# A post-norm decoder layer on one core: heads rotated and mixed in pairs, the rotated sum and its low part moved to GpSimd

## What is computed

```
x = layernorm(x + attention(x))      # 16 query heads, 4 key/value heads of 128, rotary q and k,
                                     # causal softmax, output projection Wo
x = layernorm(x + wkv(x, ctx))       # a scan along the 256 rows: running max, two decayed sums
x = layernorm(x + ffn(x))            # dense 512x512 plus top-2 of 16 rank-16 experts
```

## Time and profile before

| | |
|---|---|
| time, median of 3 runs | 1857.01 us (1853.22 to 1861.23) |
| the profiled execution's own time | 1865.38 us |
| its span, first to last instruction | 1863.6 us |
| mean granted TensorE clock | 0.962 |
| matmuls in the span | 11648 |

### The profile page before, as it was taken

The page is one execution under the profiler, slowest core; times in us unless marked ns, Lnnn a source line. Parts: engine busy times, 40 slices in busy tenths (PEclk is TensorE's granted clock), DMA queues, the critical chain, the costliest instruction groups (busy, mean ns, idle before and its releaser), DMA issues. The chain is left out here.

```text
span 1863.6 us, 36120 instructions
## 1 busy us (share of the span) xinstructions
PE 1679.0 (90%) x11648; PEld 1528.0 (82%) x11648; DVE 1612.3 (87%) x3953; ACT 1069.2 (57%) x2994; POOL 914.3 (49%) x889
## 2 busy tenths in 40 slices
PE   5899989998989898989998989899999884789998
PEld 4788988897989897988898889898888873677786
DVE  4666799899999999898999998989999988799887
ACT  4677766666666666666676666666666662121111
POOL 2333465547564655555546555655566544133221
PEclk8899999999999999999999999999999996889999
DMA  7565335223532353225312531254124412111211
GB/s 239 191 211 173 112 96 169 87 66 103 168 94 65 94 171 103 64 82 168 117 52 84 176 120 52 74 173 132 54 73 152 143 57 74 57 46 68 80 69 46
DMA packets 108554, 202.95 MB, mean 109 GB/s; under 512 B 16848, under 2 KB 58320, under 8 KB 108368
## 3 DMA queue, kind: packets, MB, share of 16 engines
q1 hardware_dynamic: 108368, 200.65, 33.6%
HBM read 120.89 MB, written 37.75 MB: 85 GB/s over the span
## 5 line engine op out<-in xcount | busy, mean ns | idle before, releaser
L759 POOL TENSOR_TENSOR RC<-QB,Cos 128x256 f32<-128x256 f32 x320 | 261.2, 816 | 577.5 <-DMA SW<-QB 476.1
L427 PE MATMUL bank<-Xh,W 128*128 128x256 f32 x1344 | 384.9, 286 | 38.1 <-DVE Xl L1035 26.4
L429 PE MATMUL bank<-Xh,W 128*128 128x256 f32 x1344 | 380.1, 283 | 0.0
L428 PE MATMUL bank<-Xl,W 128*128 128x256 f32 x1344 | 379.6, 282 | 0.0
L647 ACT ACTIVATE S<-S,NM 128x128 f32<-128x128 f32 (+1 forms) x512 | 229.0, 448 | 146.6 <-DVE NM L871 145.8
L427 PEld LDWEIGHTS bank<-Xh,W 128*128 128x128 f32 x1344 | 258.7, 192 | 41.7 <-DVE Xl L1035 30.3
L760 POOL TENSOR_TENSOR RSN<-SW,Sin 128x256 f32<-128x256 f32 x320 | 272.9, 853 | 0.0
L429 PEld LDWEIGHTS bank<-Xh,W 128*128 128x128 f32 x1344 | 259.4, 193 | 0.0
L428 PEld LDWEIGHTS bank<-Xl,W 128*128 128x128 f32 x1344 | 258.6, 192 | 0.0
L616 ACT ACTIVATE S<-S,RL 128x128 f32<-128x128 f32 (+1 forms) x512 | 203.6, 447 | 41.2 <-DVE RL L901 39.4
L427 PE MATMUL bank<-PTh,Vh 128*128 128x256 f32 (+1 forms) x512 | 138.1, 270 | 92.3 <-DVE OTl L866 91.9
(11 more groups left out here) (136 smaller groups left out, 4779.6 us busy)
## 6 DMA issues: line engine op xcount, KB each, us to landing
W<-kept SPq DMA_DIRECT2D x140, 512.0 KB, 3.6
SW<-QB SPq DMA_DIRECT2D x640, 64.0 KB, 2.0
kept<-W SPq DMA_DIRECT2D x40, 512.0 KB, 3.8
KVT<-in_wraw SPq DMA_DIRECT2D x40, 256.0 KB, 3.5
XR<-in_xt SPq DMA_DIRECT2D x16, 512.0 KB, 4.3
RO<-in_xn SPq DMA_DIRECT2D x16, 512.0 KB, 3.5
KVT<-in_ctxt SPq DMA_DIRECT2D x16, 512.0 KB, 5.0
mixed<-RO SPq DMA_DIRECT2D x16, 512.0 KB, 4.0
```

The source lines that it names most:

```text
L427: nc.tensor.matmul(dst, lhs[0], rhs[0], start=first, stop=False)
L428: nc.tensor.matmul(dst, lhs[0], rhs[1], start=False, stop=False)
L429: return nc.tensor.matmul(dst, lhs[1], rhs[0], start=False, stop=last)
L759: gp.tensor_tensor(RC[:, r % 2, :], QB[:, r % 2, :], Cos[:, :], ALU.mult)
```

## The change

Query heads are handled in pairs (`pair_of`), key tiles in pairs of a position. Per unit, ACT still writes `QB`; new is that DVE makes `RC` straight from PSUM, `(projection + bias) * Cos` (`scalar_tensor_tensor`). Once per pair SP swaps both heads with two DMAs of double size, POOL multiplies `SW` by Sin in place over both heads, adds it to `RC`, ACT rounds the pair, and POOL subtracts to make the low part. DVE's add and its subtraction of the rotated head are gone. PV is one group of 3 matmuls of 512 and 3 of 256 columns per pair, its high and low part one ACT and one DVE instruction per pair; the low part now stands first in DVE's odd slots. The lags become S 4, T 5, PT 6, PV 8, OT and WO 9. Extras stand in all odd slots (K in 1 and 3, V in 5 and 7). The position's sum is read in slot m = 1. The key tiles' swap buffers lie in the buffer `XR` of the next x, so x is loaded in slot m = 6 after the keys' sum, and split in slot 0. Tails and FFN steps start two slots later.

The diff, cut to its core:

```diff
-L_ROPE, L_SUM, L_S, L_T, L_PT, L_PV, L_WO = 1, 2, 3, 4, 5, 6, 7
-L_OTL = L_WO
+L_S, L_T, L_PT, L_WO = 4, 5, 6, 9
+L_SUM, L_Q, L_PV, L_OT = 2, 3, 8, 9
 L_ACC = HEADS - 1 + L_WO + 1
+K_SUM, K_SPLIT = 5, 6
...
-TAIL_AT = [t for i in range(PAIRS) for t in (32 * i + 31, 32 * i + 47)]
+TAIL_AT = [t for i in range(PAIRS) for t in (32 * i + 33, 32 * i + 49)]
...
+def pair_of(n, lag):
+    i = n - lag
+    return i // 2 if i % 2 == 0 and 0 <= i < ALL else None
+def next_pos(n, m):
+    s = n // HEADS + 1
+    return s if n % HEADS == m and 0 <= s < POS else None
...
         @block.sync
+                i = pair_of(n, 1)
+                if i is not None:
+                    sp.wait_ge(q_biased, 2 * i + 2)
+                    above(sp, q_summed, i)
+                    sp.dma_start(SW[0:64, :, :], QB[64:128, :, :]).then_inc(q_swapped, 16)
+                    sp.dma_start(SW[64:128, :, :], QB[0:64, :, :]).then_inc(q_swapped, 16)
...
         @block.tensor
                 g = head_of(n, L_S)
-                    pe.wait_ge(rope_lo, ROPE["Q", g] + 1)
+                    pe.wait_ge(q_lo, g // 2 + 1)
+                    if g % HEADS == 0:
+                        pe.wait_ge(k_lo, g // HEADS + 1)
+                i = pair_of(n, L_PV)
+                    pe.wait_ge(pt_lo, 2 * i + 2)
+                    above(pe, ot_lo, i)
+                    three(ot_ps[:, :, :], vs[0], [a[:, :, 0:T] for a in PT], True, False)
+                    three(ot_ps[:, :, P:T], vs[1], [a[:, :, T:T + P] for a in PT], False, True).then_inc(mixed_v, 1)
                 g = head_of(n, 0)
+                    proj_free("Q", g, 0)
                 g = head_of(n, L_WO)
-                    pe.wait_ge(ot_lo, g + 1)
+                    pe.wait_ge(ot_lo, g // 2 + 1)
...
         @block.scalar
+                i = pair_of(n, L_OT)
+                    act.wait_ge(mixed_v, i + 1)
+                    nc.scalar.activation(OT[0][:, :, :], ot_ps[:, :, :], ACT.Identity, bias=Bv[:, hf, j:j + 1]).then_inc(ot_hi, 1)
+                i = pair_of(n, L_Q)
+                    act.wait_ge(q_summed, i + 1)
+                    above(act, scored, 2 * i)
+                    copy(Q[0][:, :, :], RC[:, i % 2, :, :]).then_inc(q_hi, 1)
...
         @block.gpsimd
-                gp.tensor_tensor(RC[:, r % 2, :], QB[:, r % 2, :], Cos[:, :], ALU.mult)
-                gp.tensor_tensor(RSN[:, r % 2, :], SW[:, r % 2, :], Sin[:, :], ALU.mult).then_inc(rotated, 1)
+                i = pair_of(n, L_SUM)
+                if i is not None:
+                    pool.wait_ge(q_swapped, 32 * i + 32)
+                    gp.tensor_tensor(SW[:, :, :], SW[:, :, :], both(Sin), ALU.mult).then_inc(q_sin, 1)
+                    pool.wait_ge(q_cos, 2 * i + 2)
+                    pool.wait_ge(q_sin, i + 1)
+                    gp.tensor_tensor(RC[:, i % 2, :, :], RC[:, i % 2, :, :], SW[:, :, :], ALU.add).then_inc(q_summed, 1)
+                i = pair_of(n, L_Q)
+                if i is not None:
+                    pool.wait_ge(q_hi, i + 1)
+                    gp.tensor_tensor(Q[1][:, :, :], RC[:, i % 2, :, :], Q[0][:, :, :], ALU.subtract).then_inc(q_lo, 1)
+                s = next_pos(n, K_SUM)
+                    gp.tensor_tensor(KSW, KSW, both(Sin), ALU.mult).then_inc(k_sin, 1)
+                    gp.tensor_tensor(KRC[:, :, :], KRC[:, :, :], KSW, ALU.add).then_inc(k_summed, 1)
+                s = next_pos(n, K_SPLIT)
+                    gp.tensor_tensor(K[1][:, s % 2, :, :], KRC[:, :, :], K[0][:, s % 2, :, :], ALU.subtract).then_inc(k_lo, 1)
...
         @block.vector
-                    v.tensor_tensor(RF[:, r % 2, :], RC[:, r % 2, :], RSN[:, r % 2, :], ALU.add).then_inc(summed, 1)
+                i = pair_of(n, L_OT)
+                    dve.wait_ge(ot_hi, i + 1)
+                    v.scalar_tensor_tensor(out=OT[1][:, :, :], in0=ot_ps[:, :, :], scalar=Bv[:, hf, j:j + 1],
+                                           in1=OT[0][:, :, :], op0=ALU.add, op1=ALU.subtract).then_inc(ot_lo, 1)
+                if n % 2 == 1:
+                    turned_lo(n)
                 sg = head_of(n, L_S)
                     dve.wait_ge(scored, sg + 1)
-                    v.scalar_tensor_tensor(out=OT[1][:, g % 2, :], in0=ot_ps[:, 0:T], scalar=Bv[:, hf, j:j + 1],
-                                           in1=OT[0][:, g % 2, :], op0=ALU.add, op1=ALU.subtract).then_inc(ot_lo, 1)
...
-                    v.tensor_tensor(dst[1], RF[:, r % 2, :], dst[0], ALU.subtract).then_inc(rope_lo, 1)
                 tail(n, 0)
+                if n % 2 == 0:
+                    turned_lo(n)
...
+                g = head_of(n, 0)
+                    dve.wait_ge(q_biased, g + 1)
+                    above(dve, q_lo, g // 2 - 1)
+                    v.scalar_tensor_tensor(out=RC[:, g // 2 % 2, g % 2, :], in0=proj_ps("Q", g, 0),
+                                           scalar=Bq[:, SEQ[g // HEADS][0], m:m + 1], in1=Cos[:, :],
+                                           op0=ALU.add, op1=ALU.mult).then_inc(q_cos, 1)
```

More of the change, by code:

```diff
@@ L234, in decoder @@
         w_hi, w_lo = sem("w_hi"), sem("w_lo")
-        w_kept = [sem(f"w_kept{i}") for i in range(NP)]
+        w_kept = [sem(f"w_kept{i}") for i in range(NP // 2)]
         w_in = [sem(f"w_in{i}") for i in range(NP)]
@@ L616, in copy @@
                 return nc.scalar.activation(dst, src, ACT.Copy, **kw)
-            def to_rotate(u, r, bias):
-                act.wait_ge(projected, u + 1)
-                if u == 0:
-                    act.wait_ge(const_in, 16 * len(CONSTS))
-                above(act, rotated, r - 1)
-                nc.scalar.activation(QB[:, r % 2, :], proj_ps[u % 2][:, 0:T], ACT.Identity, bias=bias).then_inc(evacuated, 1)
             def slot(n):
                 m = n % HEADS
+                i = pair_of(n, L_OT)
+                if i is not None:
+                    act.wait_ge(mixed_v, i + 1)
+                    above(act, wo_done, 2 * i)
+                    hf, j = SEQ[2 * i // HEADS][0], 2 * i % HEADS // GROUP
+                    nc.scalar.activation(OT[0][:, :, :], ot_ps[:, :, :], ACT.Identity, bias=Bv[:, hf, j:j + 1]).then_inc(ot_hi, 1)
+                s = next_pos(n, 0)
+                if s is not None and x_first(s) is not None:
+                    b = x_first(s)
+                    act.wait_ge(x_in, 16 * b + 16)
+                    if b >= 2:
+                        act.wait_ge(q_projected, n)
+                    copy(X[0][:, XBUF[s], :, :], XR[:, :, :]).then_inc(x_hi, 1)
                 g = head_of(n, L_PT)
@@ L652, in slot @@
                     hf = SEQ[g // HEADS][0]
-                    to_rotate(UNIT["Q", g], ROPE["Q", g], Bq[:, hf, m:m + 1])
-                g = head_of(n, L_PV)
-                if g is not None:
-                    act.wait_ge(mixed_v, g + 1)
-                    above(act, wo_done, g - 1)
-                    hf, j = SEQ[g // HEADS][0], g % HEADS // GROUP
-                    nc.scalar.activation(OT[0][:, g % 2, :], ot_ps[:, 0:T], ACT.Identity,
-                                         bias=Bv[:, hf, j:j + 1]).then_inc(ot_hi, 1)
+                    act.wait_ge(q_projected, g + 1)
+                    above(act, q_swapped, 32 * (g // 2))
+                    nc.scalar.activation(QB[:, g % 2, :], proj_ps("Q", g, 0), ACT.Identity, bias=Bq[:, hf, m:m + 1]).then_inc(q_biased, 1)
                 e = extra_of(n)
@@ L663, in slot @@
                     kind, tile, s = e
-                    if kind == "V":
-                        act.wait_ge(projected, UNIT[e] + 1)
-                        above(act, mixed_v, HEADS * (s - 1))
-                        copy(V[0][:, s % 2, tile, :], proj_ps[UNIT[e] % 2][:, 0:T]).then_inc(evacuated, 1)
-                    else:
-                        to_rotate(UNIT[e], ROPE[e], Bk[:, SEQ[s][0], tile:tile + 1])
+                    if kind == "K":
+                        act.wait_ge(k_projected, JL * s + tile + 1)
+                        above(act, k_swapped, 32 * s)
+                        if s == 0 and tile == 0:
+                            act.wait_ge(const_in, 16 * len(CONSTS))
+                        nc.scalar.activation(KB[:, tile, :], proj_ps(*e), ACT.Identity,
+                                             bias=Bk[:, SEQ[s][0], tile:tile + 1]).then_inc(k_biased, 1)
+                    else:
+                        act.wait_ge(v_projected, TT * s + tile + 1)
+                        above(act, mixed_v, HEADS // 2 * (s - 1))
+                        copy(V[0][:, s % 2, tile, :], proj_ps(*e)).then_inc(v_hi, 1)
                 tail(n, 0)
```

268 lines of the change are left out of this document (126 added, 142 removed).

## The result

Over four runs of each the changed kernel takes 1926.69 us in the median (1918.63 to 1931.35), the kernel before 1859.12 in the same session. The ratio is 1.0357 [1.0304, 1.041]: slower, where 1785 was forecast. The profiled execution took 1929.09 us with a span of 1927.3 and a mean granted clock of 0.945 (before: 1863.6 and 0.962).

A forecast was written before the change was run, and what follows sets the result against it. It took PE and DVE both to bound, in different slots. Per position 47.3 - 3.1 - 1.0 (PV) + 0.75 + 0.8 - 0.25 = 44.5; 27 positions give 76, the first four 4, ends +8: 1857 - 72 = 1785 us, range 1738 to 1836.

The forecast's parts named there:

- POOL's stall: POOL late with the pair's low part behind its tail work: 3 us once per 4 positions, 0.75 a position.
- The start and the end: Scores begin one slot later, WO, tails and FFN two: +4 us at each end, +8 in all.
- the sum's first term: In each position of the steady stretch, PE's 3.1 us of waits go from the 47.3 us.
- `RO` term: WO of a position's first head waits for DVE's readout in odd slot 1: 0.3 to 2 us, taken as 0.8.
- A (no waits left): DVE's slack absorbs tails and readout, POOL is always in time; 4.5 us less a position, 1737 us; chance 20%.
- D (3%): DVE's products wait for ACT's copy ahead of the reciprocals and DVE idles in order; within 0.5% of before; chance 3%.
- B: Longer POOL operations block two-input DVE tail work, 77 us; waits stay 3.1 a position, most gain given back: 1834; chance 17%.
- C: POOL becomes the bound, its 512-column operations with a repeated operand costing up to 2.53 us; slower, 1870 to about 1955; chance 10%.
- The rule of the Trainium skill: Two-SBUF-input DVE and SBUF-reading GpSimd instructions exclude each other; others don't contend: new products run free, tail work is blocked.
- pitch: Spacing of PE's matmuls in the steady stretch: 0.25 us less a position, for a steadier PE.

The follow-up runs named there:

- i3: The kernel before, from slot 24 on DVE makes only 16 of 256 columns of both the rotated heads' low parts and their sums: 1818.46 us, 0.9744.
- g2: The kernel before with half of the tails' scans and the operations between them left out: 1776.6 us, 0.9538.
- f1: The changed kernel with the next position's value tiles projected in slots 6 and 7 in place of 5 and 7: 1917.57 us, 1.0287.
- e4: The kernel before with one more wait: DVE waits for ACT's biased copy ahead of its reciprocals: 1873.55 us, 1.0044.
- e1: The changed kernel, but DVE's cosine product reads the projection first and ACT's biased copy second: 1937.12 us, 1.0404.
- e10: As e9, and DVE's product from the projection ahead of ACT's copy: 1920.67 us, 1.031 against the kernel before.
- e8: The changed kernel with DVE's `PTl` behind the masks in odd slots too: 1897.96 us, 1.0165.
- e9: The changed kernel with the masks first in all of DVE's slots, `OTl` and `PTl` behind them: 1894.34 us, 1.0166.
- e2: The changed kernel with DVE's `PTl` ahead of the masks in even slots too: 2006.97 us, 1.0766.
- f3: As f2, with POOL's output bias adds in slot 3 of a position in place of 5: 1892.51 us, 1.0171.
- f2: As f1, with DVE's masks ahead of `OTl` and `PTl` in all slots: 1917.82 us, 1.0301.
- f4: As f3, with tails and FFN steps one slot later: 1891.33 us, 1.0154.
- g4: As f1, but PV's mixing, rounding and low part per head again, `OTl` and `PTl` placed as in the kernel before; paired rotation kept: 1973.45 us, 1.0577.
- e3: The changed kernel with DVE's later tail parts ahead of the product and the reciprocals, not at the slot's end: 1993.38 us, 1.0682.
- h1: The changed kernel, but in even slots ACT makes the exponentials ahead of the rounding `PTh`: 1949.61 us, 1.0478.
- g1: The changed kernel with half of the tails' scans and the operations between them left out: 1852.43 us, 0.9934 against the kernel before.
- i1: The kernel before, from slot 24 on DVE makes only 16 of 256 columns of the rotated heads' low parts: 1847.46 us, 0.9909.

## Why the prediction was wrong

**What held.** DVE's busy time is 1361 for 1320, POOL's 1037 for 1028. The new operations cost what was said: the product 482 ns for 478, the paired `OTl` 745 for 740, POOL's 512 columns for the heads, with the zero stride and in place, 1.30 to 1.42 for 1.35. From the changed kernel's groups by shape:

```profile
L898 DVE SCALAR_TENSOR_TENSOR OTl<-bank,Bv,OTh 128x512 fp32r<-128x512 f32 x128 | 95.4, 745 | 76.0 <-ACT OTh L646 76.0
L937 DVE SCALAR_TENSOR_TENSOR RC<-bank,Bq,Cos 128x256 f32<-128x256 f32 x256 | 123.5, 482 | 232.8 <-ACT QB L682 232.8
L787 POOL TENSOR_TENSOR SW<-SW,Sin 128x512 f32<-128x512 f32 x128 | 181.9, 1421 | 228.5 <-DMA SW<-QB 228.4
L794 POOL TENSOR_TENSOR Ql<-RC,Qh 128x512 fp32r<-128x512 f32 x128 | 166.1, 1298 | 257.7 <-ACT Qh L637 257.5
```

PV of a pair takes 1.06 by the starts (907.87 to 908.93) for 1.04. POOL's stall is bunched as forecast, 21.6 of its 25.7 us in slot 16 of 32, 0.95 a position for 0.75. The start and the end cost 14 for 8. One reading of the earlier trace rows is swapped in the prediction: by PE's order the 1.37 from 903.27 is Q and the 1.47 from 905.28 the extra, so a plain slot is 4.42 and not 4.52. The sum does not use it.

**The step that failed** is the sum's first term, "47.3 - 3.1 of waits": less work on DVE, so no PE waits. Two things are wrong with it.

First, it is too large even without a new wait. i3 takes off 144 us, half of the forecast's 292, and 26 of the 84.8 us of idleness go; at that rate the whole would take 53 of them (an estimate from i3 alone). g2 takes off 92 us in the bursts and 46 of idleness go. An engine at 91% that also ends nearly every wait looked like a bound by throughput. In part it was one by latency: a list in fixed order that shares each slot with ACT, and is late when a burst stands before what is wanted.

Second, and larger, the new waits. Forecast were 0.75 (POOL) and 0.8 (`RO`), 1.55 a position; measured are 153.9 / 27 = 5.7. `RO` alone is 1.8: it lies in the place I had named, for the reason I had named, at over twice the price. `PTl` before the transposes (1.7) and `OTl` before WO (1.2) were priced at nothing. They are used in the slot that makes them, but so they were before, where `PTl` cost 8.6 us in all; what failed is that I took no term for what the change puts ahead of them. For `PTl` f1 shows most of it: with the values' extra out of slot 5, where ACT had to stand until PV of slot 6, its wait falls from 46.8 to 5.5. For `OTl` the slot shown above has it: 6.9 us of tail work ahead of it, and f1, where it rises to 71.3 in two slots of 32, shows that it takes over what other waits give up. The mean for the `RO` term came from one slot's timeline; the wait is made by the slots with a burst, and these I had read only as durations.

**The rivals.** A (no waits left) fails by the same step. D (3%) had the mechanism nearest to what the traces show, DVE idling in order behind ACT's copy, but priced it within 0.5%; alone in the old kernel it is worth 8 us (e4), and turning it round did not help (e1, e10). B is visible in the slot shown above: four `A` took 4.59 us beside POOL's operations, their mean went from 543 to 832 ns and that of `MX` from 723 to 1029. But the tail's other operations became faster (`AD` 1052 to 476 ns, `PS` 1093 to 823), so as a total it did not come. C is wrong: POOL is busy 54%. The rule of the Trainium skill that the prediction weighed (SBUF — State Buffer, Who interferes with whom) agrees with all of this, product and paired `OTl` running at steady prices; it bears on durations, and durations were not what failed.

**The size of the miss.** A position takes 49.35 us for 44.5. Of these 4.85, 4.2 are waits (5.74 for 1.55) and 0.65 is pitch: +0.4 for -0.25, with a PE that idles more, not less, and a lower granted clock (0.96 for 0.98). 27 times that is 131 of the 140 us between 1927 and 1787, the 1859 of the same comparison less the forecast's 72; the rest is at the ends.

**Its cause, as far as it is shown.** Undone one by one, the place of `PTl` ahead of the masks is worth 36 us (e8, e9; 76 the other way, e2), the bias adds' slot 24 (f3 against f2), the values' buffer 13, at the edge of the noise (f1). They don't add up, since behind each mended wait the next comes forward: all together give 38 (f4), and 29 remain over the kernel before, besides what the lighter DVE and PV should have given. By g4 that remainder comes with the paired rotation and its lags and slots, not with PV. What in it does it stays open. These did not help: the order of product and copy (e1, e10), the tail ahead of the product (e3), its parity (f4), ACT's rounding behind the exponentials (h1). Halving the bursts helps both kernels alike (g1, g2). The one pair buffer of the weights makes ACT wait 166.9 us until PV has read it, but it cannot be all: in g4 that wait is gone and the loss is larger. Not tried are a slot more for the two low parts before their use, a product that does not share the slot's projection with ACT's copy, and the paired rotation's longer chain without its other moves.

## What to carry to other kernels

An engine's busy share in a list of fixed order, with partners that answer within the slot, is no measure of what relief is worth: DVE went from 87% to 71% busy and the kernel got 3.6% slower. Before moving work off such an engine, shorten that work in the old kernel and see what the time gives back (here 0.19, 0.5 or 0.93 us per us, by where it stood), and then list for each new or moved operation who uses it, how many slots later, and what stands ahead of it, in its engine's list and in its partner's: one used in its own slot will be found by the longest burst. An operation put ahead of the one that the partner engine waits for (here the masks) can cost all of its own time although the engine is idle elsewhere (e2: 76 us for 70 us of `PTl`), but need not (`OTl` there cost nothing); only a run tells.

## What was not expected of the hardware

A VectorE operation that meets one of GpSimd may last as long as that one, whatever its own size. In i1 a low part of 16 columns took 1.41 us; DVE and POOL in that moment:

```profile
901.39 1.41 DVE L889 TENSOR_TENSOR Ql<-RF,Qh 128x16 fp32r<-128x16 f32 x1
...
906.51 0.46 DVE L889 TENSOR_TENSOR Ql<-RF,Qh 128x16 fp32r<-128x16 f32 x1 [0.81 <-ACT Qh L616]
```

```profile
900.28 2.49 POOL L790 TENSOR_TENSOR E<-E,KVT 128x1024 f32<-128x1024 f32 x1 [0.62 <-DVE QS L974]
```

The first ended at 902.80, as POOL's 1024-column operation did (902.77). So part of DVE's "busy" time in the kernel before was waiting for POOL, counted as work: 526 of the 772 ns of a head's low part remain at a sixteenth of its columns, while the keys' low parts fell to 196. At the 0.41 us of a quick one the 256 low parts of the heads would have taken 105 us in place of 197.6 (an estimate). A busy share hides such waits.
